# An audio tower on one core: engine orders rewritten, shorter root iterations, row hats moved to ScalarE, and setup transfers redistributed

## Chip, cores and metric

The kernel runs on 1 core of a Trainium2 chip. The metric is the device time of one execution in microseconds (us). All arithmetic that matters here is float32.

## The reference, cut to what matters

x is (128, 750, 64). Three layers follow one another; each adds to a running h of shape (128, 47, 128).

```python
# tokens: deformable convolution over w = 46 words of K = 16 taps
off  = einsum('bwkc,ock->bow', xr, w_off) + b_off
dy, dx = off[:, 0::2], off[:, 1::2]
px   = base + dx;  x0 = floor(px);  frac = px - x0
v0, v1 = gather(x0), gather(x0 + 1)                  # zero outside the row
wy   = maximum(0, 1 - abs(dy))
val  = wy * ((1 - frac) * v0 + frac * v1)
h    = concat(cls, einsum('bckw,dck->bwd', val, w_def) + b_def) + positional
# attention, one head of 128, over S = 47 tokens, on z = layernorm(h)
est  = einsum('bqkh,h->bqk', tanh(hq[:, :, None] + hk[:, None] + b1), W2[0]) + b2
h    = h + softmax(Q K^T / sqrt(128) + est) V
# experts: top 2 of 8 and a shared one, on z = layernorm(h)
h    = h + sum_e combine_e * (relu(z w1_e + b1_e) w2_e + b2_e) + relu(z sw1 + sb1) sw2 + sb2
```

The layer norm divides by sqrt(var + 1e-5). The two experts of a token are the two of highest score, ties going to the lower number.

## The kernel before, in words

The 128 sequences are cut into 16 units of 8. A unit goes through a pipeline of pieces, and at one time different units are at different stages. An engine has a list of pieces (`ORDER`) that it runs once per step; `AHEAD` says how many units ahead of (or behind) the step s the unit is on which a piece works: a, p, q, y take unit s+3, t and x unit s+4, h unit s+2, b, c, k, n unit s+1, m unit s, r unit s−1, f, g, d unit s−2. Each engine runs its list in order; between engines only semaphores hold.

The pieces that the text speaks of:

- x0 (SP) loads x of a unit, in 16 transfers (line 288). t0 to t3 (VectorE, line 535) transpose it, a3 (TensorE, line 793) makes the offsets, a3 (ScalarE, line 404) copies them out of PSUM, a4 (TensorE, line 800, the selection matmul) spreads them, and a4 (VectorE, `stage_a`, lines 543 to 563) transposes them and makes row positions, gather indices (line 551) and interpolation weights.
- GpSimd issues 36 indirect gathers per unit (line 382) for six of the eight sequences, in three blocks of 12, into one of two buffers G. c0, c1, c2 (VectorE, lines 597 to 618) combine one block each. Line 597 copies the weights to PSUM.
- The other two sequences are done without a gather: p0 (SP) writes the positions to memory, q0 (SP) reads them back spread over the partitions (PXB, WYB), h0 to h3 and k0 to k3 (ScalarE, lines 413 and 420) make hat functions of them, n0 to n3 (TensorE, line 818) multiply them with plain rows (XN, loaded by y0 on SP), and n0, n1 (VectorE, line 632, `dense_out`) scale the result.
- b3 (TensorE, line 779, sixteen matmuls, "the projection") makes the tokens of all eight sequences; b3 (VectorE, lines 642 and 643) adds the position code and gives h0.
- m0 to m5 are the first layer norm and the attention scores; m51, m52 the tanh estimates, written to memory and read back as SC by e0, e1, e2 (SP, lines 326 and 333). r6, r7 are the softmax (VectorE lines 665 to 672, ScalarE line 463), r7, r8 (TensorE) transpose and multiply by the values, r9 to r12 the second layer norm and the gate, r13 (VectorE, lines 693 to 699) the ranks of the experts, r14 the combine weights, gc their transposition.
- m1 and r10 (VectorE, `rstd`, lines 570 to 577) are the reciprocal square root of the variance: a shift of the bits gives a first value, three Newton rounds of three small instructions each refine it.
- For each expert f (TensorE line 940, ScalarE line 494) makes the hidden rows through one PSUM bank, g (TensorE line 951, VectorE line 728) scales them, d (TensorE line 963) adds them up; fs and ds are the shared expert; d8, d9 add, transpose and store the result.

The lists before:

```python
"tensor": gc n0 fs g0 n1 m0 f0 ds f1 m1 r7 f2 g1 r8 d0 m2 g2 r9 m3 f3 g3 m4 r10 m5 f4 g4 m51 d1 r11 f5 n2 g5 m52 n3
          r12 d2 f6 g6 d3 b3 f7 g7 a3 d4 a4 d5 d6 d7 d8
"scalar": gc k0 fs r6 f0 m0 f1 r7 k1 f2 k2 m3 r9 f3 m41 m4 m5 f4 m51 k3 f5 h0 m52 h1 r12 h2 f6 h3 f7 a3
"vector": r6 c0 r7 g0 m1 g1 r8 m2 n0 g2 m3 m4 g3 r10 g4 c1 r11 g5 c2 n1 r12 r13 g6 r14 b3 g7 t0 t1 a4 d8 t2 d9 t3
"sync":   x0 e0 e1 e2 p0 q0 y0 d9
```

At the start SP loads x of unit 0 and later all large constants, ScalarE's queue loads the six small ones (identity, offset weights, row bases and the like), and TensorE makes two products of attention matrices (lines 988 to 990) before it begins the first projection. GpSimd's program has a loop over pairs of units, and so has SP's.

Of the kernel before, what the change touches and what calls it, by code (L numbers as in the profile page):

```python
# [6 lines left out]
K = 16  # L7
# [30 lines left out]
ROUND = 8388608.0  # L38

CONSTS = [  # L40
    ("ident", [128, 128]), ("wof", [128, KP * 32]), ("selm", [128, 128]), ("base", [128, NBLK * 4]),
    ("boff", [128, 8]), ("rowbase", [128, GBLK]),
# [13 lines left out]
    "tensor": ("gc n0 fs g0 n1 m0 f0 ds f1 m1 r7 f2 g1 r8 d0 m2 g2 r9 m3 f3 g3 m4 r10 m5 f4 g4 m51 d1 r11 f5 n2 g5 m52 n3 "  # L56
               "r12 d2 f6 g6 d3 b3 f7 g7 a3 d4 a4 d5 d6 d7 d8").split(),
    "scalar": ("gc k0 fs r6 f0 m0 f1 r7 k1 f2 k2 m3 r9 f3 m41 m4 m5 f4 m51 k3 f5 h0 m52 h1 r12 h2 f6 h3 f7 a3").split(),
    "vector": ("r6 c0 r7 g0 m1 g1 r8 m2 n0 g2 m3 m4 g3 r10 g4 c1 r11 g5 c2 n1 r12 r13 g6 r14 b3 g7 t0 t1 a4 d8 t2 d9 t3").split(),
    "sync": ("x0 e0 e1 e2 p0 q0 y0 d9").split(),  # L60
}

END_ORDER = {}
# [9 lines left out]
class Chain:  # L73


    def __init__(self, eng, sem):
        self.eng, self.sem, self.base, self.n = eng, sem, 0, 0

    def __call__(self, ins):
        ins.then_inc(self.sem, 1)  # L80
        self.n += 1
        self.eng.wait_ge(self.sem, self.base + self.n)

    def mark(self):
        self.at = self.n

    def loop(self, i, first, per):

        self.outer = self.base + self.n
        self.base, self.n = self.outer + (i - first) * per, 0  # L90

    def end(self, trips, per):
        assert self.n == per, (self.n, per)
        self.base, self.n = self.outer + trips * per, 0


def audio_tower(nc, x, consts, rows, pw, est, out):
# [4 lines left out]
    with ctx:  # L102
# [21 lines left out]
        ones = sb("ones", [128, 128])  # L124
# [56 lines left out]
        eq = sb("eq", [RT, RN, E, E])  # L181
# [20 lines left out]
        def cols(t):  # L202
            return bank[t][:, 0:COLS]
# [13 lines left out]
        x_turned, off_full, off_ready, ot_full, ot_read, idx_ready, pw_ready = (  # L217
            sem(n) for n in ("x_turned", "off_full", "off_ready", "ot_full", "ot_read", "idx_ready", "pw_ready"))
# [18 lines left out]
        def early(engine, pieces, s):  # L237

            for name in ORDER[engine]:
                v = s + AHEAD[name[0]]  # L240
                if name in pieces and 0 <= v < UNITS:
                    pieces[name](v // 2, v % 2)

        def steps(eng, engine, pieces, chain=None, last=(UNITS - 4) // 2, loop=True):

            def step(i, t):
                for name in (END_ORDER.get(t, ORDER) if isinstance(i, int) else ORDER)[engine]:
                    v = t + AHEAD[name[0]]
                    if not isinstance(i, int):
                        pieces[name](i + v // 2, v % 2)  # L250
                    elif 0 <= v < UNITS:
                        pieces[name](v // 2, v % 2)

            if not loop:
                for s in range(-1, UNITS + 2):
                    step(0, s)
                return
            for s in (-1, 0, 1, 2):
                step(0, s)
            if chain:  # L260
                chain.mark()
            for s in (3, 4):
                step(0, s)
            per = chain.n - chain.at if chain else 0
            with eng.Fori(2, last) as i:
                if chain:
                    chain.loop(i, 2, per)
                for r in (1, 2):
                    step(i, r)
            if chain:  # L270
                chain.end(last - 2, per)
            for s in range(2 * last + 1, UNITS + 2):
                step(0, s)
# [4 lines left out]
        def _(sp):  # L278
# [16 lines left out]
            def write_positions(m, h):  # L295
# [3 lines left out]
                for r, t in ((0, nw[:, GBLK:NBLK, :]), (1, offs[:, GBLK:NBLK, 4:8])):  # L299
# [44 lines left out]
            load_x(0, 0)  # L344
# [4 lines left out]
            early("sync", pieces, -3)  # L349
            for name, _s in CONSTS[NFIRST + 1:]:  # L350
                sp.dma_start(cs[name][:, :], consts[name]).then_inc(const_in, 16)
            sp.wait_ge(zeroed, 1)
            for b in range(NB):
                sp.dma_start(w2blk[H * b:H * b + H, b:b + 1], rows["w2col"]).then_inc(blk_in, 16)
            early("sync", pieces, -2)
            steps(sp, "sync", pieces, last=(UNITS - 6) // 2)
# [4 lines left out]
        def _(pool):  # L361
            pool.memset(w2blk[:, :], 0.0).then_inc(zeroed, 1)
# [5 lines left out]
            pool.memset(ones[:, :], 1.0).then_inc(zeroed, 1)  # L368
# [18 lines left out]
            gathers(0, 0)  # L387
# [671 lines left out]
```

## Time and profile before

| | us |
|---|---|
| median of 3 runs | 860.05 (859.48 to 864.42) |
| the profiled execution, its own time | 864.31 |
| its span on the core | 862.5 |
| VectorE busy | 670.7 |
| TensorE busy (matmul) | 691.1 |
| ScalarE busy | 515.8 |
| GpSimd busy | 547.7 |

The span is that of the profiled execution from its first to its last instruction. Busy times leave out semaphore and DMA-issuing instructions and the short gaps between dependent ones. The mean granted TensorE clock was 0.956 of full speed.

### The profile page before, as it was taken

How to read it: one execution, taken by the hardware profiler on the slowest of the kernel's cores; microseconds unless marked ns; L12 is line 12 of the kernel's file. 1: busy time of each engine (PE TensorE's matmuls, PEld its weight loads, DVE VectorE, ACT ScalarE, POOL GpSimd, SP SyncE). 2: the span in 40 equal slices, each digit the busy share in tenths (PEclk: the TensorE clock that was granted, in tenths of full speed). 3: DMA queues.
4: the chain of work that ended last, by engine and by line, in shares of the span. 5: the costliest groups of instructions: out<-in, count | busy, mean ns of one | idle time of the engine just before them, and what ended most of it. 6: DMA issues, size and time to landing. Idle time of an engine off the chain costs nothing.

```text
span 862.5 us, 17862 instructions
## 1 busy us (share of the span) xinstructions
PE 691.1 (80%) x6294; PEld 416.1 (48%) x6294; DVE 670.7 (78%) x1750; ACT 515.8 (60%) x903; POOL 547.7 (63%) x588
## 2 busy tenths in 40 slices
PE   2106586879899898989898988888888999998786
PEld 0004354545465555555464645555554555555342
DVE  5146667879888988898898989898888889796552
ACT  0217565647675857767576758585775767744422
POOL 1777777777777777777777777777777777300000
PEclk9999978899989998999999999999999999999889
DMA  4877486647373747565564647475756354200101
GB/s 145 183 180 192 88 170 137 125 84 176 58 206 61 186 86 154 118 123 143 100 169 57 197 76 170 101 155 117 138 131 125 73 93 99 44 18 10 27 0 19
DMA packets 130669, 97.79 MB, mean 113 GB/s; under 512 B 87180, under 2 KB 118868, under 8 KB 130588
## 3 DMA queue, kind: packets, MB, share of 16 engines
q1 hardware_dynamic: 111292, 58.64, 26.3%
q0 software_dynamic: 18432, 37.79, 25.7%
q8 instruction: 50, 0.82, 0.4%
q10 hardware_dynamic: 864, 0.30, 0.1%
q14 instruction: 31, 0.25, 0.1%
HBM read 88.75 MB, written 7.90 MB: 112 GB/s over the span
## 4 chain that ended last, share of the span: by engine, by line
DVE 41%; PE 37%; issue 9%; ACT 5%; SPq 4%; DMA 3%; DVEq 0%; ACTq 0%
PE bank L779 8%; PE bank L940 6%; PE bank L818 5%; DVE XT L535 4%; PE bank L963 4%; DVE bank L609 4%; DVE VAL L615 4%; PE bank L854 3%; DVE G L606 3%; DVE TH L654 3%; DVE VT L632 3%; PE bank L793 2%; DVE GE L728 2%; ACT HT L413 2%; SPq L288 2%
## 5 line engine op out<-in xcount | busy, mean ns | idle before, releaser
L382 POOL DMA_INDIRECT G<-in_x,idx x576 | 545.4, 947 | 195.7 <-issue 173.7
L413 ACT ACTIVATE HT<-PXB,c_lneg 128x736 f32<-128x736 f32 x192 | 160.1, 897 | 74.4 <-PE bank L818 55.5
L818 PE MATMUL bank<-HT,XN 128*32 128x184 f32 x3072 | 137.9, 329 | 8.5 <-ACT HT L420 5.2
L940 PE MATMUL bank<-Z,c_w1e 128*128 128x376 f32 x288 | 125.9, 519 | 20.3 <-ACT HE L494 18.4
L420 ACT ACTIVATE HT<-HT 128x2208 f32<-128x2208 f32 x64 | 130.3, 2036 | 0.6
L818 PEld LDWEIGHTS bank<-HT,XN 128*32 128x32 f32 x3072 | 102.8, 113 | 42.7 <-issue 17.5
L779 PE MATMUL bank<-VT,c_wdef 128*128 128x380 f32 x256 | 87.2, 495 | 23.2 <-DVE VT L632 23.2
L963 PE MATMUL bank<-GE,c_w2e 128*128 128x376 f32 x256 | 104.4, 513 | 0.7 <-DVE GE L728 0.7
L535 DVE STREAM_TRANSPOSE XT<-xt 128x768 f32<-128x768 f32 x64 | 59.9, 958 | 54.2 <-DMA xt<-in_x 33.3
L494 ACT ACTIVATE HE<-bank,c_fb 128x376 f32<-128x376 f32 x128 | 73.0, 570 | 38.9 <-PE bank L940 37.2
L728 DVE TENSOR_TENSOR GE<-HE,bank 128x376 f32<-128x376 f32 x128 | 68.7, 537 | 34.4 <-ACT HE L494 24.7
L779 PEld LDWEIGHTS bank<-VT,c_wdef 128*128 128x128 f32 x256 | 48.1, 193 | 61.5 <-DVE VT L618 28.5
L940 PEld LDWEIGHTS bank<-Z,c_w1e 128*128 128x128 f32 x288 | 49.7, 193 | 57.4 <-ACT HE L494 31.4
L963 PEld LDWEIGHTS bank<-GE,c_w2e 128*128 128x128 f32 x256 | 45.1, 198 | 31.5 <-issue 17.5
L609 DVE TENSOR_TENSOR bank<-G,bank 128x384 f32<-128x384 f32 x96 | 54.0, 562 | 3.3
L615 DVE TENSOR_TENSOR VAL<-G,bank 128x384 f32<-128x384 f32 x96 | 53.1, 553 | 3.3
L793 PE MATMUL bank<-XT,c_wof 128*32 128x384 f32 x256 | 26.5, 536 | 30.3 <-DVE XT L535 20.3
L463 ACT ACTIVATE SC<-SC,smx 47x47 f32<-47x47 f32 x128 | 40.8, 320 | 16.5 <-DVE smx L667 16.5
L618 DVE STREAM_TRANSPOSE VT<-VAL 128x768 f32<-128x768 f32 x48 | 47.0, 978 | 1.7
L606 DVE TENSOR_TENSOR G<-G,bank 128x768 f32<-128x768 f32 x48 | 45.4, 945 | 0.6
L951 PE MATMUL bank<-cT,selb 72*128 72x376 bf16 x128 | 43.5, 340 | 0.3 <-DVE GE L728 0.2
L834 PE MATMUL bank<-h,c_center 128*128 128x376 f32 x64 | 29.1, 536 | 16.7 <-DVE smx L667 16.7
(136 smaller groups left out, 931.3 us busy)
## 6 DMA issues: line engine op xcount, KB each, us to landing
xt<-in_x SPq DMA_DIRECT2D x256, 96.0 KB
PXB<-pw SPq DMA_DIRECT2D x16, 768.0 KB
G<-in_x,idx POOLq DMA_INDIRECT x576
XN<-in_x SPq DMA_DIRECT2D x16, 384.0 KB
est<-SQHC SPq DMA_DIRECT2D x32, 141.0 KB
WYB<-pw SPq DMA_DIRECT2D x64, 48.0 KB
out<-OUTS SPq DMA_DIRECT2D x64, 44.0 KB
SC<-est SPq DMA_DIRECT2D x16, 69.0 KB
```

The costliest lines, as they stand in the source:

```text
L382: pool.indirect_dma_start(out=G[h][:, col, :], out_offset=None, in_=x.rearrange("b (l c) -> (b l) c", c=C), in_offset=bass.IndirectOffsetO ...
L413: act.activation(HT[half][:, c, :, :].rearrange("p g (w n) -> p g w n", n=4), PXB[h][:, :].rearrange("p (g w i n) -> p i g w n", g=NG, i=2 ...
L420: act.activation(rows_, rows_, ACT.Relu, bias=1.0, scale=-1.0).then_inc(hat_ready, 1)
L494: act.activation(HE[e % 4][:, :], cols(2), ACT.Relu, bias=cs["fb1"][:, e:e + 1]).then_inc(he_ready, 1)
L535: dve.transpose(XT[:, :, 96 * bp:96 * bp + 96].rearrange("p q (t i) -> p t q i", i=32), xt[:, WG * bp:WG * bp + WG, :].rearrange("p t (q i ...
L609: ins = dve.tensor_tensor(prod, G[h][:, k0 + a:k0 + b, C:2 * C], weight(1, a, b), ALU.mult)
L615: chain(dve.tensor_tensor(VAL[:, a:b, :], G[h][:, k0 + a:k0 + b, 0:C], prod, ALU.add))
L728: dve.tensor_tensor(GE[e % 4][:, :], HE[e % 4][:, :], cols(3), ALU.mult).then_inc(ge_ready, 1)
L779: mm = pe.matmul(bank[0][:, 0:TOK], wdef[:, q, :], VT[:, q, :], start=(q == 0), stop=(q == KP - 1))
L818: mm = pe.matmul(bank[0][32 * g:32 * g + 32, HW * c:HW * c + HW], XN[h][:, b, C * ch + 32 * c:C * ch + 32 * c + 32], HT[half][:, k, g, :], ...
L940: pe.matmul(cols(2), w1e[:, e, :], Z2[h][:, :], start=True, stop=True).then_inc(up_full, 1)
L963: pe.matmul(cols(4), w2e[:, e, :], HS[:, 0:COLS] if e == E else GE[e % 4][:, :], start=(e == E), stop=False).then_inc(down_done, 1)
```

## The change

1. The helpers for loops go; each engine's steps are written out, GpSimd's and SP's too.
2. All four lists have a new order.
3. `rstd`: another first guess and constants; after one round of three instructions comes one of four.
4. `stage_a`: the bias of the offsets is added by ScalarE in its copy (`Identity` with bias); the hat functions for the gathered rows go to ScalarE as a new piece a4 (`row_hats`, five activations); the sign of nw turns. The product of the weights is made in c0 straight into PSUM, in place of the copy.
5. Ranks: one comparison against a constant `least` (0 or the smallest positive number, by the place of the pair) replaces an equality, a mask and a comparison. The maximum of the softmax is negated by the reduction.
6. Setup: x of unit 0 is loaded half by SP, half by ScalarE's queue; the six small constants by GpSimd's queue; the large constants and the attention vector (29 transfers) by ScalarE's queue after its first step. The products of attention matrices come after the first projection.

```diff
 ORDER = {
+    "tensor": ("n0 fs gc g0 n1 f0 ds m0 f1 m1 r7 d0 g1 f2 r8 m2 g2 f3 m3 r9 g3 m4 d1 r10 m5 f4 m51 d2 g4 f5 m52 r11 g5 n2 "
+               "f6 r12 g6 d3 f7 g7 d4 d5 n3 d6 b3 d7 d8 a3 a4").split(),
+    "scalar": ("gc fs r6 f0 m0 k0 f1 r7 f2 k1 f3 m3 r9 m41 m4 m5 f4 m51 f5 m52 k2 f6 r12 k3 h0 h1 f7 h2 h3 a3 a4").split(),
+    "vector": ("r6 c0 r7 g0 m1 g1 r8 m2 n0 g2 m3 g3 m4 r10 g4 c1 r11 g5 r12 g6 c2 n1 r13 g7 r14 b3 d8 d9 a4 t0 t1 t2 t3").split(),
+    "sync": ("x0 y0 e0 e1 e2 p0 d9 q0").split(),
 }
...
+            def row_hats(m, h):
+                u = 2 * m + h
+                act.wait_ge(ot_read, u + 1)
...
+                act.activation(nw[h][:, :, :], offT[:, :, 0:4], ACT.Abs).then_inc(nw_abs, 1)
+                act.wait_ge(nw_abs, u + 1)
+                act.wait_ge(rest_ready, u + 1)
+                act.activation(nw[h][:, :, :], nw[h][:, :, :], ACT.Relu, bias=1.0, scale=-1.0).then_inc(pw_ready, 1)
+                for i in range(2):
+                    act.activation(e01[h][:, :, :, i], rest[:, :, :], ACT.Abs, bias=float(i)).then_inc(e_abs, 1)
+                act.wait_ge(e_abs, 2 * u + 2)
+                e = e01[h][:, :, :, :].rearrange("p t n s -> p (t n s)")
+                act.activation(e, e, ACT.Relu, bias=1.0, scale=-1.0).then_inc(e_ready, 1)
...
-                chain(dve.tensor_tensor(offs[:, :, :], offT[:, :, 0:8], cs["boff"][:, :].unsqueeze(1).broadcast_to([128, NBLK, 8]), ALU.add))
-                chain(dve.tensor_tensor(offs[:, :, 4:8], offs[:, :, 4:8], base, ALU.add))
-                pxg = offs[:, 0:GBLK, 4:8]
+                chain(dve.tensor_tensor(px[:, :, :], offT[:, :, 4:8], base, ALU.add))
+                pxg = px[:, 0:GBLK, :]
...
+                wait(dve, e_abs, 2 * u)
+                dve.scalar_tensor_tensor(rest[:, :, :], rr[:, :, :], ROUND, pxg, ALU.subtract, ALU.subtract).then_inc(rest_ready, 1)
...
-                    for _i in range(3):
-                        chain(dve.scalar_tensor_tensor(nt_[:, :], ry[:, :], -0.5, ry[:, :], ALU.mult, ALU.mult))
-                        chain(dve.tensor_tensor(nt_[:, :], nt_[:, :], var[:, :], ALU.mult))
-                        chain(dve.scalar_tensor_tensor(ry[:, :], nt_[:, :], 1.5, ry[:, :], ALU.add, ALU.mult))
+                    chain(dve.scalar_tensor_tensor(nt_[:, :], ry[:, :], -0.703952253, ry[:, :], ALU.mult, ALU.mult))
+                    chain(dve.tensor_tensor(nt_[:, :], nt_[:, :], var[:, :], ALU.mult))
+                    chain(dve.scalar_tensor_tensor(ry[:, :], nt_[:, :], 1.68191391, ry[:, :], ALU.add, ALU.mult))
+                    chain(dve.tensor_tensor(nt_[:, :], ry[:, :], ry[:, :], ALU.mult))
+                    chain(dve.tensor_tensor(nt_[:, :], nt_[:, :], var[:, :], ALU.mult))
+                    chain(dve.scalar_tensor_tensor(nt_[:, :], nt_[:, :], -10.0 / 3.0, nt_[:, :], ALU.add, ALU.mult))
+                    chain(dve.scalar_tensor_tensor(ry[:, :], nt_[:, :], 5.0, ry[:, :], ALU.add, ALU.mult))
...
-                chain(dve.reduce_max(smx[:, :], SC[:, :, 0:S], AX.X))
-                dve.tensor_scalar(smx[:, :], smx[:, :], -1.0, None, ALU.mult).then_inc(sc_ready, 1)
+                dve.tensor_reduce(smx[:, :], SC[:, :, 0:S], AX.X, ALU.max, negate=True).then_inc(sc_ready, 1)
...
-                chain(dve.scalar_tensor_tensor(eqv, gtv, 0.0, cs["tri"][0:RT, :].unsqueeze(1).broadcast_to([RT, RN, E * E]),
-                                               ALU.is_equal, ALU.mult))
-                chain(dve.scalar_tensor_tensor(gtv, gtv, 0.0, eqv, ALU.is_gt, ALU.add))
+                chain(dve.tensor_tensor(gtv, gtv, least[:, :].unsqueeze(1).broadcast_to([RT, RN, E * E]), ALU.is_ge))
...
-            early("tensor", pieces, -3)
-            early("tensor", pieces, -2)
+            steps("tensor", pieces, -3, 0)
```

## Rows read from the trace of the kernel before

**Rows 1.** The page's busy time of each engine, share, instructions.
```profile
PE 691.1 (80%) x6294; PEld 416.1 (48%) x6294; DVE 670.7 (78%) x1750; ACT 515.8 (60%) x903; POOL 547.7 (63%) x588
```
**Rows 2.** Timeline of GpSimd: start, us, what; first and last gather.
```profile
22.42 1.09 POOL L382 DMA_INDIRECT G<-in_x,idx  x1 [19.59 <-DVE idx L551]
...
742.95 0.94 POOL L382 DMA_INDIRECT G<-in_x,idx  x1 [0.30 <-issue]
```
**Rows 3.** Stretches between projections: length, busy us by engine, clock, DMA.
```profile
core 0: us, PE busy (x) PEld busy (x) DVE busy (x) ACT busy (x) POOL busy (x), PEclk, DMA share, GB/s
263.31:309.69 46.38, 40.95 (x393) 24.65 (x394) 41.18 (x109) 31.93 (x56) 35.10 (x38) 1.00 0.58 129
309.69:358.54 48.85, 43.94 (x393) 26.88 (x394) 41.48 (x109) 32.03 (x56) 36.96 (x40) 0.93 0.58 126
...
404.93:452.35 47.42, 42.30 (x394) 26.05 (x394) 41.39 (x109) 32.06 (x56) 35.84 (x39) 0.96 0.61 132
```
**Rows 4.** Timeline of TensorE, four places.
```profile
123.38 5.35 PE L779 MATMUL bank<-VT,c_wdef 128*128 128x380 f32 x16 [1.08 <-DVE VT L632]
...
411.70 1.50 PE L793 MATMUL bank<-XT,c_wof 128*32 128x384 f32 x16 [0.63 <-DVE h L643]
...
413.87 0.91 PE L800 MATMUL bank<-off,c_selm 128*128 128x384 f32 x2
...
772.96 5.34 PE L779 MATMUL bank<-VT,c_wdef 128*128 128x380 f32 x16 [1.45 <-DVE VT L632]
...
778.93 2.69 PE L963 MATMUL bank<-GE,c_w2e 128*128 128x376 f32 x8
```
**Rows 5.** VectorE's waits, 200 to 700 us: total, times, longest.
```profile
DVE GE L728 <- ACT HE L494: 15.1, 11, 1.4
DVE XT L535 <- PE bank L793: 12.4, 10, 1.2
```
**Rows 6.** Groups by line: busy us, mean ns, idle before.
```profile
L696 DVE SCALAR_TENSOR_TENSOR eq<-gt,c_tri 94x256 f32<-94x256 f32 x16 | 7.0, 437 | 0.5
...
L546 DVE TENSOR_TENSOR offs<-offT,c_boff 128x96 f32<-128x96 f32 x16 | 4.2, 262 | 0.5
...
L476 ACT ACTIVATE eg<-lg 94x32 f32<-94x32 f32 x16 | 3.7, 229 | 37.6 <-DVE lg L685 37.6
...
L556 DVE TENSOR_SCALAR nw<-nw 128x48 f32<-128x48 f32 x16 | 3.0, 188 | 0.6
...
L498 ACT ACT_TABLE_LOAD x1 | 1.3, 1283 | 4.3 <-issue 4.3
```
**Rows 7.** Timeline of VectorE within one step, 421 to 448 us.
```profile
421.85 0.56 DVE L665 SCALAR_TENSOR_TENSOR SC<-bank,c_b2col,SC 47x376 f32<-47x376 f32 x1
...
428.71 0.15 DVE L570 TENSOR_SCALAR var<-bank 94x4 f32<-94x4 f32 x1
...
431.27 0.55 DVE L577 TENSOR_TENSOR diag<-c_ident,ry 94x376 f32<-94x376 f32 x1
...
447.13 0.94 DVE L606 TENSOR_TENSOR G<-G,bank 128x768 f32<-128x768 f32 x1
```
**Rows 8.** Timeline of the start, SP's queue and VectorE.
```profile
0.76 10.41 SPq L288 DMA_DIRECT2D xt<-in_x  x16
...
6.64 0.23 DVE L525 CAST identb<-c_ident 128x128 bf16<-128x128 f32 x1 [1.43 <-DMA c_rowbase<-in_rowbase]
...
13.21 0.98 DVE L535 STREAM_TRANSPOSE XT<-xt 128x768 f32<-128x768 f32 x1 [1.05 <-DMA xt<-in_x]
```
**Rows 9.** Estimates: SP's timeline in a step, and the last read in the chain.
```profile
448.22 1.06 SPq L326 DMA_DIRECT2D est<-SQHC  x2
454.91 0.28 SPq L333 DMA_DIRECT2D SC<-est  x1
...
806.71 5.83 DMA SC<-est
```

More of the change, by code:

```diff
@@ L81, in __call__ @@
         self.n += 1
[L82 to L94, printed above, removed]
+        self.eng.wait_ge(self.sem, self.n)
 def audio_tower(nc, x, consts, rows, pw, est, out):
@@ L123, in audio_tower @@
         b2s = sb("b2s", [72, 128], bf16)
-        ones = sb("ones", [128, 128])
+        spread = sb("spread", [128, 128])
         mean1 = sb("mean1", [128, 1])
@@ L136, in audio_tower @@
         offT = sb("offT", [128, NBLK, 32])
-        offs = sb("offs", [128, NBLK, 8])
-        nw = sb("nw", [128, NBLK, 4])
+        px = sb("px", [128, NBLK, 4])
+        nw = [sb(f"nw{p}", [128, NBLK, 4]) for p in range(2)]
+        rest = sb("rest", [128, GBLK, 4])
         rr = sb("rr", [128, GBLK, 4])
-        e01 = sb("e01", [128, GBLK, 4, 2])
-        e01f = e01[:, :, :, :].rearrange("p t n s -> p (t n s)")
+        e01 = [sb(f"e01{p}", [128, GBLK, 4, 2]) for p in range(2)]
         rowb = sb("rowb", [128, GBLK])
         idx = [sb(f"idx{p}", [128, GBLK * 4], i32) for p in range(2)]
-        aw = [sb(f"aw{p}", [128, GBLK, 4, 2]) for p in range(2)]
         G = [sb(f"G{p}", [128, GBLK * 4, 2 * C]) for p in range(2)]
@@ L235, in audio_tower, with load_first, steps @@
         dve_chain, act_chain = sem("dve_chain"), sem("act_chain")
[L237 to L273, printed above, removed]
+        def load_first(eng, parts):
+            for bp in parts:
+                src = x[bass.ds(2 * bp, 2), :].rearrange("b (t w g n) -> g w b t n", t=WG, w=16, g=NG)
+                for g in range(NG):
+                    eng.dma_start(xt[32 * g:32 * g + 32, WG * bp:WG * bp + WG, :], src[g]).then_inc(x_in[bp], 16)
+        def steps(engine, pieces, first, last):
+            for s in range(first, last):
+                for name in ORDERS.get(s, ORDER)[engine]:
+                    u = s + AHEAD[name[0]]
+                    if name in pieces and 0 <= u < UNITS:
+                        pieces[name](u // 2, u % 2)
         block = ctx.enter_context(nc.Block())
@@ L348, in _ @@
                       "e0": write_estimate(0), "e1": write_estimate(1), "e2": read_estimate}
[L349 to L356, printed above, removed]
+            steps("sync", pieces, -3, UNITS + 2)
             for h in range(2):
@@ L367, in _ @@
             pool.memset(HS[:, :], 0.0).then_inc(zeroed, 1)
-            pool.memset(ones[:, :], 1.0).then_inc(zeroed, 1)
+            pool.memset(spread[:, :], 0.375).then_inc(zeroed, 1)
             pool.memset(mean1[:, :], 1.0 / D).then_inc(zeroed, 1)
@@ L385, in gathers @@
                         ).then_inc(gathered[h][bp], 16)
-            gathers(0, 0)
-            gathers(0, 1)
-            with pool.Fori(1, UNITS // 2) as i:
-                gathers(i, 0)
-                gathers(i, 1)
+            for u in range(UNITS):
+                gathers(u // 2, u % 2)
         @block.scalar
@@ L766, in _ @@
             dve.wait_ge(dve_consts, 5)
+            chain(dve.tensor_scalar(least[:, :], cs["tri"][0:RT, :], -TINY, TINY, ALU.mult, ALU.add))
             for p in range(2):
@@ L853, in piece @@
                     pe.wait_ge(diag_ready[ln], 2 * m + h + 1)
-                    pe.matmul(cols(LNB[ln]), ones[0:RT, :], diag[ln][:, :, :].rearrange("p t r -> p (t r)"),
+                    pe.matmul(cols(LNB[ln]), spread[0:RT, :], diag[ln][:, :, :].rearrange("p t r -> p (t r)"),
                               start=True, stop=True).then_inc(rstd_full[ln], 1)
@@ L991, in _ @@
             pe.wait_ge(setup_mats, 5)
-            steps(pe, "tensor", pieces, loop=False)
+            steps("tensor", pieces, 0, UNITS + 2)
 def kernel(**inputs):
```

77 lines of the change are left out of this document (37 added, 40 removed).

## The prediction

> **What bounds the kernel now.** I read five views, in this order: the busy shares, GpSimd's timeline from end to end, the table of stretches cut at the token projection (TensorE's sixteen matmuls of line 779, once per unit, a good mark for one step), VectorE's waits, and one step instruction by instruction.
>
> By the busy shares TensorE has 80%, VectorE 78%, GpSimd 63% [rows 1]. GpSimd's share misleads. It issues 576 gathers; the first starts at 22.42 and the last at 742.95 [rows 2], so one comes every (742.95 − 22.42) / 575 = 1.253 us, of which only some 0.95 counts as busy. 36 gathers a unit make 45.0 us a unit: a floor under every step that no other engine can beat, and it runs nearly without a break. A step takes 46.38 us where the granted clock was 1.00, and 47.42 and 48.85 us at 0.96 and 0.93 [rows 3]. So the engines run 1.4 us a unit behind what GpSimd would allow, and the lost time piles up: the projection of unit 1 starts at 123.38, that of unit 15 at 772.96 [rows 4], that is 649.6 us for 14 units, 46.4 each.
>
> Who sets the 46.38? VectorE is busy 41.18 us of it and some 100 small gaps between dependent instructions fill most of the rest; over 200 to 700 us it waits 15.1 us in 11 places for the experts' hidden rows and 12.4 us in 10 for the offset matmuls [rows 5], that is 2.6 us a step. TensorE is busy 40.95 us of the same step [rows 3]. So VectorE's instruction list is the bound of a step (43.8 us occupied), TensorE second (about 41), GpSimd third only in appearance: its 45.0 is a hard floor.
>
> **The change, part by part, per unit.**
> *Offsets and hats (line 543 to 563).* Seven VectorE instructions go: the bias add (0.262 us), the two of nw, four of e01; the cheapest, line 556, takes 0.188 [rows 6]. Seven at about 0.225, with 0.03 us from each end to the next start, give 1.8 us. The weights' product of line 563 takes the place of the copy of line 597, at the same price. ScalarE gets five activations of 36 to 96 elements; the nearest, 32 elements, takes 0.229 us [rows 6], so 1.2 us on an engine that is busy 31.93 of 46.38 us [rows 3]. They run after the last transposition of a step, and next behind them on ScalarE stand the copy of the combine weights and the shared hidden rows, whose matmuls are due 3 us later: hidden; without that cover 1.2 us.
> *Roots.* Twelve small instructions run from 428.71 to 431.27 [rows 7], 0.213 us each. Three rounds (9) become two of higher order (3 + 4): two fewer, 0.43 us, twice a unit: 0.86.
> *Ranks and maxima.* One 94x256 instruction goes, 0.437 us [rows 6], and the negation: 0.47 + 0.2. The comparison, written as a plain two-tensor operation, and the two products of line 632 have no reason to be dearer: nothing.
> Sum on VectorE: 1.8 + 0.86 + 0.67 = 3.3 us of 43.8, leaving 40.5. TensorE loses nothing. If all of it came off the step, a step would be 43.1 us, below GpSimd's 45.0: at least 1.9 of the 3.3 us can't show.
>
> *The new orders.* They decide the rest; I cut a step in two.
> Stretch one, from the start of the projection to VectorE's first softmax instruction, now 404.93 to 421.85: 16.9 us [rows 3, 7]. After the change: projection 5.34 [rows 4]; VectorE's adds of h0 0.8; offset matmuls, ScalarE's copy and the selection matmul 411.70 to 414.78 = 3.1 us [rows 4]; then stage_a 1.9 us (seven instructions instead of fourteen), and only then all four transposes of x, of which two now stand ahead of it and cover the offsets' round trip; they are 0.98 us each, 0.9 apart [rows 8]: 3.6. Sum 14.75, so 2.2 saved, though VectorE now idles about 2 us in front of stage_a, with the four transposes behind it.
> Stretch two, from there to the next projection: 46.38 − 16.9 = 29.5 us at full clock. Off: 0.2 + 0.43 + 0.43. On: the gate's maximum and one expert's product move from behind the third gather block to ahead of it, 0.87. Net −0.2. Today this stretch has hardly a wait at full clock [rows 5]. Walking the new lists I find new ones: VectorE at r8, because ScalarE's first hats (2.5 us) now stand ahead of f1 and of the copy that TensorE's r8 needs: 0.75; at g4, since TensorE does d2 first: 0.5; at m2 and r12 0.4. Bounds 0 and 2.5; I take 1.7, as each rests on durations of this trace. So 14.75 + 29.3 + 1.7 = 45.7 against 46.38: 0.7 us a step, ends 44.0 (then GpSimd's 45.0 holds) and 46.5. Of the 3.3 us removed 2.6 turn into waits for TensorE. The steps at a lower clock (47.42, 48.85 us) cost as much more as now: TensorE's work is the same.
>
> *Start.* The first gather waits for the first indices. x comes in 16 transfers on one queue, issued over 10.41 us, and the last block is turned at 13.21 [rows 8]; half of them on ScalarE's queue take up to 5 us off that. Against it, the constants that VectorE waits for, now there at 6.6 us, go through GpSimd's queue; nothing in the trace prices a plain transfer from there. Between 0 and 4 us earlier, I take 1.5. The Trainium skill, "DMA: Bandwidth & Descriptors", section "Specifications", gives the GpSimd path about 1 us to the first byte against 0.6 for the others; by that alone six transfers would hold the start back by about 2 us and leave less of the gain; no run here shows it yet. The 29 setup transfers move from SP to ScalarE (some 14 us of issue), behind unit 0's offsets and ahead of its hats, which wait that long for the positions to be written out and spread (PXB): hidden, and unit 0 has slack anyway, as its third gather block is not in before 67 us. Without that cover they would cost 14 us once. The setup matrices move behind the first projection; that frees TensorE's first dense matmuls.
> But the second unit is bound by GpSimd: 72 gathers end at 22.4 + 90.2 = 112.6, plus landing (0 to 5.8 us, the SC read below being the longest near; I take 2), plus 5.2 us from the third block to the projection (447.13 to 452.35 [rows 3, 7]) is 119.8, less 1.5 = 118.3 against 123.38. Unit 2 likewise: 163.4 against 168.4. Gain there 5 us, no more.
>
> *End.* Behind unit 15's projection TensorE still has eight matmuls of expert products (778.93, 2.69 us) that hold the output add and then the softmax [rows 4]; in the new order they come first: 2.5 us. Two softmax, root and rank passes shorter by 0.2 + 0.43 + 0.47 lie bare there: 1.5. Together 4.
>
> *Sum.* 5 (start) + 12 x 0.7 (units 2 to 14) + 1.5 (last short step) + 4 (end) = 19 us. Span 862.5 − 19 = 843.5; its own time 864.3 − 19 = 845.3. The median, 860.05, lies 4.3 below that execution, so I forecast 841.
>
> *The clock.* A rule that speaks against denser work: stretches of the same 393 matmuls took 46.38 us at 1.00 and 48.85 at 0.93 [rows 3], so the clock falls now and then to the lower of its levels, 1.2 GHz, in the middle of full work. The Trainium skill, "TensorE: Matmul & The Clock Gate", section "HAM oscillation — how this bites in real kernels", says that regular stalls between bursts make the clock drop again and again. By it new waits of TensorE (at r7, for the first gather block, 3 us) could cost a dip in every step, 1.0 to 2.5 us; by the rows, where TensorE idles 5.4 us of the 46.38 and keeps the full clock, nothing changes. I go by the rows.
>
> *Tables.* ScalarE's copy of the offsets becomes an Identity with a bias. One table load in the whole run, 1.283 us [rows 6]. Were Identity outside the loaded set, two loads a unit would lie on the offsets' round trip: 2.6 x 16 = 41 us. The Trainium skill, "ScalarE: Activation LUTs", section "Table sets: the hidden batching unit", says that identity, copy, relu and abs are in every set. I give the loads 1 in 100.
>
> **The rivals.**
> *GpSimd takes over (20%).* If the new waits are nearer 0.7 than 1.7, every step falls to 45.0. Then unit 15's third block starts when its last gather is in: 742.95 + 0.94 + 2 − 1.5, less GpSimd's one wait of some 1 us, about 743.3; projection 748.5 instead of 773.0; with the end's 4 that is −28.5: 831.5. For it: each wait in the walk is half a microsecond's difference between long sums. Against it: all of them would have to be wrong on the same side.
> *All of it becomes waits (17%).* Step 46.4 as before, only start and end gain: 860 − 8 = 852. For it: the offsets' round trip lies bare on VectorE, and TensorE must be waited for after the projection.
> *The estimate's round trip, slower than before (6%).* SP's y0 (the load of XN) now stands ahead of e0, e1, e2, and it waits for n1, late in the step. So the write and read of the estimates start only there: 0.5 + 1.1 (two writes, 448.22), 5.6 us until the read is issued (454.91), and 5.8 us until it lands [rows 9]: 13.0 us, while VectorE wants them 14.75 us after n1. It decides from 14.75 on: each us more per step costs 12 to 13 us. With 3 us more, as loaded queues could bring, 841 + 38 = 879. Today the writes go out 4 us before the projection (448.22 against 452.35). Against it: the heavy loads of x are over by then.
>
> **How the numbers follow.** Forecast 841 has 55%, with 837 to 848 as its own range; the rest (2%) is tables and the unforeseen. The range reaches down to the rival of GpSimd, 831, and up past 852 to a step 0.3 us longer, 857. A measurement of this kernel tells 1% (8.6 us) from nothing. Faster by more: 0.55 + 0.20 + a little of the second rival = 0.78; within: 0.15; slower: 0.07.
>
> **What would show it.** Step length at full clock 45.7 (45.0: first rival; 46.4: second); VectorE busy down by some 48 us to about 620, with waits before stage_a (2 us each) in place of the hidden-row waits; GpSimd's first gather near 21 and its last near 741.5; unit 15's projection near 758; no wait of the softmax add for the SC read (third rival: one in each step). I am wrong if that wait appears, if ScalarE's five activations hold TensorE at the shared rows, or if there is more than one table load.

## The result: slower by 1.25%, and the profile after

The changed kernel took 872.47 us (median, 869.75 to 875.39), the kernel before 860.91 on the same chip (859.48 to 865.72): a ratio of 1.0125, interval 1.0103 to 1.0148. The forecast was 841 us, with a range up to 857. The profiled execution after has a span of 870.7 us against 862.5, 8.2 more.

The page's busy time of each engine (it answers to [rows 1]):

```profile
PE 704.6 (81%) x6294; PEld 412.8 (47%) x6294; DVE 628.7 (72%) x1543; ACT 535.8 (62%) x983; POOL 553.4 (64%) x594
```

VectorE lost 42 us (forecast 48) and the run became longer: the first sign that VectorE's work wasn't what the time came from. Next the table of stretches cut at the token projection, now line 748 (beside [rows 3]):

```profile
268.41:314.80 46.39, 41.40 (x394) 24.17 (x394) 38.76 (x96) 33.14 (x62) 35.06 (x37) 1.00 0.71 129
412.05:458.08 46.03, 41.40 (x393) 24.17 (x394) 38.88 (x96) 33.12 (x62) 34.85 (x37) 1.00 0.63 130
458.08:507.21 49.13, 44.18 (x394) 26.45 (x394) 38.56 (x96) 33.26 (x62) 37.14 (x40) 0.93 0.62 125
603.12:653.56 50.44, 44.48 (x394) 26.03 (x394) 38.71 (x96) 33.25 (x62) 35.94 (x39) 0.93 0.61 120
```

A step at full clock takes 46.0, hardly less than the 46.38 of before, and the slowest 50.44. Marks along the run show where the 8.2 us arose. The projection of unit 3 starts at 219.33 (before 214.72): 4.6 late. The ten steps from there to 699.55 take 480.2 (before 471.6, 214.72 to 686.28): 8.7 more. The next two take 88.1 against 86.7: 1.4 more. From unit 15's projection to the end there are 83.05 us (787.65 to 870.7), before 89.5: 6.5 less. The sum is +8.2.

VectorE's waits from 200 to 700 us (total, times, longest; beside [rows 5]):

```profile
DVE offT L521 <- PE bank L769: 19.8, 10, 2.0
DVE h L650 <- PE bank L881: 10.7, 6, 2.3
DVE h L616 <- PE bank L748: 10.1, 10, 1.1
DVE GE L698 <- PE bank L920: 9.0, 10, 1.2
...
DVE SC L639 <- DMA SC<-est: 6.8, 6, 1.9
```

The first line is the offsets' round trip that no transpose covers, 1.98 us in each step, forecast as 2. The last is the wait that the prediction named as a sign that it is wrong. One step, first SP's timeline, then VectorE's (start, us, what; they answer to [rows 9] and [rows 7]):

```profile
411.93 0.40 SPq L284 DMA_DIRECT2D XN<-in_x  x1
412.38 1.05 SPq L292 DMA_DIRECT2D est<-SQHC  x2
420.47 0.25 SPq L299 DMA_DIRECT2D SC<-est  x1
```

```profile
421.43 0.58 DVE L521 STREAM_TRANSPOSE offT<-bank 128x384 f32<-128x384 f32 x1 [1.98 <-PE bank L769]
...
423.23 3.56 DVE L512 STREAM_TRANSPOSE XT<-xt 128x768 f32<-128x768 f32 x4
427.00 0.60 DVE L639 SCALAR_TENSOR_TENSOR SC<-bank,c_b2col,SC 47x376 f32<-47x376 f32 x1 [0.21 <-DMA SC<-est]
...
619.71 0.60 DVE L639 SCALAR_TENSOR_TENSOR SC<-bank,c_b2col,SC 47x376 f32<-47x376 f32 x1 [1.93 <-DMA SC<-est]
```

From y0 to the addition pass 427.00 − 411.93 = 15.07 us; from the first write to the issue of the read 8.09, before 6.69 [rows 9]. Over the whole run this wait makes 13.0 us in 9 places.

The start, from four timelines (GpSimd's first constant and last constant, VectorE, GpSimd's first gather; beside [rows 8] and [rows 2]), and two places of unit 0 and unit 1:

```profile
1.27 0.72 POOL L322 DMA_DIRECT2D c_wof<-in_wof  x1 [0.82 <-POOLq L1016]
...
4.11 0.56 POOL L323 DMA_DIRECT2D c_ident<-in_ident  x1
```

```profile
10.65 0.23 DVE L502 CAST identb<-c_ident 128x128 bf16<-128x128 f32 x1 [5.45 <-DMA c_ident<-in_ident]
...
116.59 0.95 DVE L580 TENSOR_TENSOR G<-G,bank 128x768 f32<-128x768 f32 x1 [2.09 <-DMA G<-in_x,idx]
```

```profile
22.14 1.01 POOL L344 DMA_INDIRECT G<-in_x,idx  x1 [15.37 <-DVE idx L528]
...
112.81 0.94 POOL L344 DMA_INDIRECT G<-in_x,idx  x1 [0.30 <-issue]
```

```profile
120.53 0.74 PE L787 MATMUL bank<-HT,XN 128*32 128x184 f32 x8 [3.12 <-ACT HT L392]
```

```profile
12.41 2.70 DVE L512 STREAM_TRANSPOSE XT<-xt 128x768 f32<-128x768 f32 x3 [0.44 <-DMA xt<-in_x]
...
124.35 0.87 DVE L606 TENSOR_TENSOR VT<-bank,WYB 128x184 f32<-128x184 f32 x2 [3.43 <-PE bank L787]
```

The identity is used at 10.65 where it was used at 6.64, and the first gather starts only 0.28 us earlier. The second transpose of x still has to wait for x at 12.41. In unit 1 TensorE's n3 waits for ScalarE's hats, and VectorE's last scaling (line 606) waits 3.43 us for TensorE, right ahead of the projection.

Last the clock, in windows of 2.5 us behind one projection (same columns as the stretches):

```profile
236.83:239.33 2.50, 0.69 (x3) 0.10 (x1) 2.36 (x5) 2.50 (x14) 1.89 (x3) 1.00 1.11 65
239.33:241.83 2.50, 2.26 (x14) 1.92 (x14) 2.40 (x7) 2.50 (x5) 1.89 (x3) 0.66 0.78 100
241.83:244.33 2.50, 2.50 (x7) 1.36 (x6) 2.19 (x11) 1.48 (x4) 1.89 (x3) 0.50 0.97 307
...
285.91:288.41 2.50, 0.94 (x3) 0.30 (x2) 2.34 (x5) 2.50 (x14) 1.89 (x2) 1.00 1.10 80
```

It falls to 0.50 (the lower of its levels, 1.2 GHz) right behind a stretch in which TensorE was busy 0.69 us of 2.50. The kernel before has the same kind of fall, behind 1.53 of 2.50 us. A thin stretch doesn't always bring a fall: at the same place of the next step (last row) TensorE is busy 0.94 of 2.50 us, and that step keeps the full clock. Of the ten middle steps three have the full clock throughout, before five.

### The profile page after: what moved, and what is told of

Read it like the earlier page. It is cut to its first block, busy times and chain, and to the rows that moved or that the text cites. A ratio compares the mean times of both kernels' runs of the same rounds, so it can differ in the third digit from the quotient of the medians.

```text
span 870.7 us, 17175 instructions
## 1 busy us (share of the span) xinstructions
PE 704.6 (81%) x6294; PEld 412.8 (47%) x6294; DVE 628.7 (72%) x1543; ACT 535.8 (62%) x983; POOL 553.4 (64%) x594
## 4 chain that ended last, share of the span: by engine, by line
PE 35%; DVE 29%; DMA 16%; issue 8%; ACT 8%; SPq 3%; DVEq 0%; ACTq 0%
DMA SC<-est 7%; DMA est<-SQHC 6%; PE bank L909 5%; PE bank L748 5%; DVE bank L583 5%; DVE VAL L589 5%; PE bank L932 4%; DVE G L580 4%; DVE XT L512 3%; PE bank L881 2%; ACT HT L385 2%; DVE GE L698 2%; PE bank L787 2%; ACT SC L435 2%; PE bank L823 2%
## 5 line engine op out<-in xcount | busy, mean ns | idle before, releaser
L909 PE MATMUL bank<-Z,c_w1e 128*128 128x376 f32 x288 | 129.8, 534 | 26.8 <-ACT HE L466 25.2
L787 PEld LDWEIGHTS bank<-HT,XN 128*32 128x32 f32 x3072 | 97.2, 114 | 74.2 <-DVE offT L521 18.6
L932 PE MATMUL bank<-GE,c_w2e 128*128 128x376 f32 x256 | 107.0, 514 | 0.0
L512 DVE STREAM_TRANSPOSE XT<-xt 128x768 f32<-128x768 f32 x64 | 57.1, 947 | 3.1 <-DMA xt<-in_x 2.6
L521 DVE STREAM_TRANSPOSE offT<-bank 128x384 f32<-128x384 f32 x16 | 9.3, 583 | 65.0 <-PE bank L769 65.0
```

What stands on the lines that cost most here:

```text
L512: dve.transpose(XT[:, :, 96 * bp:96 * bp + 96].rearrange("p q (t i) -> p t q i", i=32), xt[:, WG * bp:WG * bp + WG, :].rearrange("p t (q i ...
L787: mm = pe.matmul(bank[0][32 * g:32 * g + 32, HW * c:HW * c + HW], XN[h][:, b, C * ch + 32 * c:C * ch + 32 * c + 32], HT[half][:, k, g, :], ...
L909: pe.matmul(cols(2), w1e[:, e, :], Z2[h][:, :], start=True, stop=True).then_inc(up_full, 1)
L932: pe.matmul(cols(4), w2e[:, e, :], HS[:, 0:COLS] if e == E else GE[e % 4][:, :], start=(e == E), stop=False).then_inc(down_done, 1)
```

## The experiments

Line numbers are those of the changed kernel except where a kernel starts from the old one. My first theory: the new lists, not the arithmetic, cost the time, through y0 ahead of the estimates and through the bare offset round trip. Its rivals: the arithmetic itself (ScalarE's hats, the added rounds), the setup, or GpSimd as the bound whatever the lists.

**First set of runs: two single orders and two crossings.** A crossing sets the lists of one kernel in the other.

```diff
 a_y0_last (changed kernel)
-    "sync": ("x0 y0 e0 e1 e2 p0 d9 q0").split(),
+    "sync": ("x0 e0 e1 e2 p0 d9 q0 y0").split(),
 b_y0_first (kernel before)
-    "sync": x0 e0 e1 e2 p0 q0 y0 d9
+    "sync": x0 y0 e0 e1 e2 p0 q0 d9
 a_old_lists: the changed kernel, all four lists of before (and a4 last on ScalarE)
 b_new_lists: the kernel before, all four new lists (without ScalarE's a4)
```

> The changed kernel with one edit: SP's list has y0 (the load of XN) last again, behind q0, instead of second. Theory 1, the estimates' round trip behind y0 costs the time: the 13.0 us of waits of VectorE's softmax add for the SC read (9 times) vanish, and with them some 10 to 13 us: 859 to 862 us. Theory 2, the lower TensorE clock (0.93 against 0.956) has its own cause, the new waits of TensorE: the waits vanish but the steps at a low clock stay: 866 to 870 us. Theory 3, the softmax waits are only where other lateness shows: no change, 871 to 873.

> The kernel before with one edit: SP's list has y0 second, ahead of e0, e1, e2. Theory 1 (the round trip is what costs): its softmax add comes 16.9 us after the projection began, 2 us later than in the changed kernel (14.9), and the round trip takes about 14 to 16 us, so hardly any wait: 861 to 864 us. If y0 ahead of the estimates hurts whatever the rest of the order, 870 us or more.

> The changed kernel with the four lists of before (ScalarE's with a4 added at its end): the arithmetic and setup changes alone. VectorE's list, 43.8 us occupied of 46.4, is shortened by 3.3 us: if the lists are at fault, a step falls to GpSimd's 45.0 us, and the time to 840 to 846 us. If the arithmetic or the setup is at fault, it stays at 860 or above.

> The kernel before with the new lists and its own arithmetic and setup. VectorE does 3.3 us more per step than in the changed kernel, of which about 1 us falls into its new wait before stage_a: if the lists are at fault it is slower than both, 890 to 910 us. If the setup or the arithmetic is at fault, about 860.

Measured against the kernel before: 1.0121, 0.9988, 0.9997 and 1.0107. None of these numbers says what it was meant to: on this chip the kernel before itself took 1574.05 us, some 93 us a step. Once in a step most engines stand still for some 46 us. Here are ScalarE and TensorE in b_y0_first, and GpSimd and ScalarE in a_asis, the unedited changed kernel on another chip of this kind (third set):

```profile
752.09 0.47 PE L818 MATMUL bank<-HT,XN 128*32 128x184 f32 x1 [2.33 <-issue]
...
753.51 2.50 ACT L413 ACTIVATE HT<-PXB,c_lneg 128x736 f32<-128x736 f32 x3 [46.39 <-remote]
```

```profile
624.17 0.95 POOL L344 DMA_INDIRECT G<-in_x,idx  x1 [49.55 <-DVE idx L528]
...
676.26 0.57 ACT L466 ACTIVATE HE<-bank,c_fb 128x376 f32<-128x376 f32 x1 [45.38 <-remote]
```

While GpSimd issues its gathers (45 us), the rest hardly moves: TensorE starts single matmuls with pauses of up to 2.33 us in which it waits for nothing that the profile shows. Then GpSimd waits as long for new indices. What releases ScalarE is called "remote", which means that the profile doesn't show it. At line 413 ScalarE reads the positions that come back from memory (PXB), but at line 466 it doesn't; so their read-back, which some expectations below blame, isn't shown to be the cause. The cause stays open. All but b_y0_first were run again.

**Second set.**

> The changed kernel with y0 last in SP's list, again, on another chip. Theory 1, the estimates' round trip behind y0: its 13 us of waits vanish and so do 10 to 13 us of the time, 859 to 862 us. Theory 2, the lower TensorE clock has its own cause, TensorE's new waits: the waits vanish, the many steps at a low clock stay, 866 to 870 us.

> The changed kernel with the four old lists, again, on another chip: arithmetic and setup alone. If the lists are at fault: steps of 45.0 us (GpSimd's floor), 840 to 846 us. If the arithmetic or the setup is: 860 or more.

> The kernel before with the new lists, again, on another chip. If the lists are at fault: slower than the changed kernel, 885 to 905 us, as VectorE still has 3.3 us more in each step. If they aren't: about 860.

Two changes of one thing each: y0, and the transposes that cover the offsets' round trip again.

```diff
 a_cover = a_y0_last, and in "vector":
-  ... r14 b3 d8 d9 a4 t0 t1 t2 t3
+  ... r14 b3 t0 t1 a4 d8 t2 d9 t3
```

> The changed kernel with y0 last and, in VectorE's list, the offsets' round trip covered again: t0 t1 a4 d8 t2 d9 t3 in place of d8 d9 a4 t0 t1 t2 t3. VectorE's 2.0 us of wait before stage_a should vanish and a full-clock step fall from 46.0 to GpSimd's 45.0 us. By theory 1: 845 to 850 us. By theory 2, which has the clock follow TensorE's waits, the gain over a_y0_last is less than 5 us.

| | us (before 868.33) | ratio | interval |
|---|---|---|---|
| a_y0_last_2 | 862.15 | 0.9944 | 0.9920 to 0.9968 |
| a_cover | 850.78 | 0.9813 | 0.9781 to 0.9844 |
| a_old_lists_2 | 845.88 | 0.9775 | 0.9739 to 0.9811 |
| b_new_lists_2 | 914.66 | 1.0564 | 1.0521 to 1.0606 |

The crossing decides. The arithmetic and the setup under the old lists gain 2.25%; the new lists under the old arithmetic lose 5.6%, more than the 885 to 905 us expected. Under the changed arithmetic the new lists cost 16.3 us on this chip (862.15 with y0 last against 845.88). Stretches of a_old_lists_2, a_cover and b_new_lists_2, one near the same place of each:

```profile
255.91:300.48 44.57, 40.93 (x394) 24.64 (x394) 38.27 (x96) 32.65 (x61) 33.59 (x37) 1.00 0.63 134
```

```profile
404.98:450.14 45.16, 41.40 (x393) 24.16 (x394) 38.46 (x96) 33.13 (x62) 34.37 (x36) 1.00 0.71 131
```

```profile
331.18:380.40 49.22, 43.00 (x394) 24.97 (x394) 42.03 (x109) 32.05 (x57) 34.06 (x36) 0.97 0.60 121
```

Under the old lists a step falls to GpSimd's floor: 45.1 us in the mean of ten (36 times 1.253 is 45.1), with single steps of 43.6 made up for by longer ones, and between 200 and 700 us GpSimd never waits for indices. Its timeline at the end and VectorE's last block of unit 15 (a_old_lists_2):

```profile
743.67 0.94 POOL L344 DMA_INDIRECT G<-in_x,idx  x1 [0.30 <-issue]
```

```profile
746.43 0.95 DVE L580 TENSOR_TENSOR G<-G,bank 128x768 f32<-128x768 f32 x1 [0.79 <-DMA G<-in_x,idx]
```

That is the rival "GpSimd takes over" in its mechanism. Its numbers were too low: unit 15's projection starts at 751.66, not 748.5, and the end is not the shorter one of the new lists, so that the gain is 22.5 us against the kernel before and not 28.5. Under the new lists with the old arithmetic no step of the middle part is under 49.2, and GpSimd waits for indices (40.1 us in 8 places between 200 and 700). The stage_a of before has fourteen instructions where the changed one has seven, and in these lists all of them lie bare behind the offsets' round trip.

a_cover against a_y0_last_2 is one move in one list: 1.3%, 11.4 us, where theory 2 allowed less than 5. So this move alone, two transposes over the offsets' round trip, brings back 11.4 of the 16.3 us. At full clock the step falls from 45.8 to 45.25 us in the mean. Part of what is won goes to a new wait: the transposes that now come early must wait until the matmuls of line 762 have read XT (16.9 us in 10 places between 200 and 700).

**Third set**, again a chip on which every version takes about twice as long (the kernel before 1565.57). The expectations were written before this was known.

```diff
 a_asis: the changed kernel, unedited
 a_old_y0 = a_old_lists with "sync": x0 y0 e0 e1 e2 p0 q0 d9
 a_best = a_old_lists, and
-ORDERS = {}
+ORDERS = {s: LATE for s in range(14, 18)}
 (LATE holds the four new lists)
 a_cover_n1 = a_cover, and in "tensor":
-  n0 fs gc g0 n1 f0 ds m0 f1 m1 r7 d0
+  n0 fs gc g0 f0 ds m0 f1 m1 n1 r7 d0
```

> The changed kernel itself, unedited, beside the others on one chip, so that what y0 costs is known on the same footing. Ratio to the kernel before 1.0125 as measured first. Against the 0.9944 of the version with y0 last that leaves 1.8%, 15.6 us, for y0's place. If the difference between chips made it, it comes nearer to 1.00.

> The old lists with the changed arithmetic, with y0 second in SP's list. Theory 1, the price of y0's place depends on how soon the softmax add comes after the projection (16 to 17 us in the old lists, 14.9 in the new ones, for a round trip of about 15 to 16): nearly free here, ratio 0.978 to 0.982. Rival: y0 costs its 1.8% in any order, as the round trip is on the path of each step: ratio 0.995.

> The old lists with the changed arithmetic in steps up to 13, and the new lists in the last four steps, where there are no more gathers to wait for. Projection of unit 15 to the end took 88.9 us with the old lists and 83.1 with the new: if that end is worth what it looks, 6 us off, ratio 0.9705, about 840 us beside 868 of before. Rival: the gain of the end was the step before it being late anyway: 0.977 as without it.

> a_cover with one edit in TensorE's list: the second dense piece n1 (2 us) moves from behind g0 to just ahead of r7, into the thinnest stretch of a step, where TensorE waits for the softmax and after which the clock was seen to fall. Theory of the clock: with the stretch filled the dips go (clock 0.95 and more, steps all near 45.2), ratio 0.970 to 0.975. Rival, the idle time only moves ahead of m0 and the dips with it: 0.981 as a_cover.

Measured: 1.0105, 0.9991, 0.9985, 0.9905. They tell nothing of the step under test: a step is made up of other waits here, and among the versions with the new lists one is 1% longer than the kernel before and one 1% shorter.

**Fourth set, the same four.**

> The changed kernel, unedited, again, on a chip where the positions are read back at the normal speed. Ratio to before 1.0125 as first measured, so that y0's place is worth 1.8% (15.6 us). If a difference between chips made it: nearer to 1.00.

> Old lists, changed arithmetic, y0 second in SP's list, again. If y0's price depends on how soon the softmax add follows the projection: 0.978 to 0.982, nearly free. If it costs 1.8% in any order: 0.995.

> Old lists up to step 13, new lists for the last four steps, again. If the new lists' end is worth its 6 us: 0.9705. If not: 0.9775.

> a_cover with TensorE's n1 moved to just ahead of r7, again. If the clock falls because of that thin stretch: 0.970 to 0.975, clock 0.95 or more. If the idle time only moves: 0.981.

| | us (before 861.36) | ratio | interval |
|---|---|---|---|
| a_asis_2 | 862.62 | 1.0012 | 0.9988 to 1.0036 |
| a_old_y0_2 | 845.61 | 0.9810 | 0.9783 to 0.9837 |
| a_best_2 | 838.96 | 0.9744 | 0.9717 to 0.9772 |
| a_cover_n1_2 | 866.18 | 1.0062 | 1.0040 to 1.0083 |

The unedited kernel is not slower here. Against it the same arithmetic under the old lists, with y0 in the same place, gains 17.0 us on the same chip (862.62 to 845.61). y0 ahead of the estimates costs the old lists some 0.35% by comparison over two chips (0.9810, 0.9775; the intervals overlap), with no wait for SC between 200 and 700 us. a_best is the fastest version: old lists up to step 13 and the new ones for the last four. From its projection of unit 15 (753.70) to the end pass 82.5 us, with the old lists throughout 88.9 (a_old_lists_2: 751.66 to 840.6): so the new order of the end is worth 6.4 us in these two traces. The times say less: 0.9744 lies between the 0.9705 and the 0.9775 that were expected, 0.3% below a_old_lists_2 on the other chip.

a_cover_n1 tests a theory of the clock: that it falls because TensorE runs thin ahead of r7, so n1's matmuls are moved there. The move made it 2.5% slower than a_cover (1.0062 against 0.9813, on two chips), with full-clock steps of 46.0 to 46.5, and more steps with a fall, not fewer. TensorE's waits from 200 to 700, a_cover first, a_cover_n1_2 second:

```profile
PE bank L909 <- ACT HE L466: 2.1, 7, 0.4
```

```profile
PE bank L909 <- ACT HE L466: 20.3, 10, 2.2
```

The idle time wasn't filled but moved ahead of f1 and grew. The theory fell in this form, its rival (0.981) too, and what sets the falls stays open.

**Fifth set: the changed kernel and y0 last, on one chip.**

> The changed kernel unedited, on the same chip as the next run, which the earlier runs of the two never were. If the place of y0 costs what the two results on different chips say (1.012 for the changed kernel on its first chip, 0.994 with y0 last on another), it is 1.8% slower than the next run; if what the second chip of the changed kernel says (1.001), 0.7%.

> The changed kernel with only y0 moved behind e0 e1 e2. Full-clock step 45.7 to 46.0 us, no wait of the softmax's addition for the estimates above 0.3 us in most steps; 0.994 of the kernel before as on its first chip. Against the changed kernel on this same chip: 0.7% faster by the one reading, 1.8% by the other; and if most of the 1.8% was the chip and not the order, the two stand within 0.5%.

Against 866.88 of before: a_asis_3 861.84, ratio 0.9960 (0.9935 to 0.9986); a_y0_last_3 860.62, 0.9945 (0.9915 to 0.9975). The two stand 0.15% apart, which can't be told from nothing: the price of 1.8% that a comparison over chips had suggested isn't there on this chip. On the first chip y0 last was never run, so what its place cost there isn't shown. SP's timeline of one step of a_asis_3, VectorE's addition behind it, and VectorE's wait for it between 200 and 700:

```profile
409.08 1.05 SPq L292 DMA_DIRECT2D est<-SQHC  x2
416.54 0.25 SPq L299 DMA_DIRECT2D SC<-est  x1
```

```profile
423.44 0.56 DVE L639 SCALAR_TENSOR_TENSOR SC<-bank,c_b2col,SC 47x376 f32<-47x376 f32 x1
```

```profile
DVE SC L639 <- DMA SC<-est: 0.9, 1, 0.9
```

Here 7.46 us pass from write to read, not 8.09, and the addition doesn't wait. Over the eleven steps from 200 to 700 us the interval is 7.0 to 7.7 (a_asis_3) and 7.1 to 8.0 (a_asis_2); in the first ten of after it was 7.4 to 8.6. The order leaves the trip hardly any slack, so half a microsecond more or less decides whether the addition waits. Two stretches of a_asis_3:

```profile
454.55:500.16 45.61, 41.40 (x393) 24.16 (x394) 38.45 (x96) 33.11 (x62) 34.51 (x37) 1.00 0.64 132
500.16:548.66 48.50, 44.30 (x394) 26.20 (x394) 38.65 (x96) 33.23 (x62) 36.62 (x40) 0.93 0.63 126
```

Of my first theory the lists stand: they take the gain, mainly by the offsets' round trip that nothing covers (a_cover). y0's place shows no price on this last chip.

## Why the prediction was wrong

**What held.** The removed work: VectorE's busy time fell by 42 us to 628.7 (forecast 48, to about 620). The 2 us ahead of stage_a, in every step. The walk through the new lists: 45.7 at full clock, measured 45.6 to 45.8 in a_asis_3, 45.6 to 46.0 in a_y0_last_2, and 46.0 to 46.4 on the first chip. Stretch one of the step shown, 427.00 − 412.05 = 14.95 (forecast 14.75). One table load. The end: 6.5 us gained, forecast 4 (its two shorter passes, at 1.1 us each, should have counted 2.2 and not 1.5).

**The step that failed: "The steps at a lower clock (47.42, 48.85 us) cost as much more as now".** I forecast the step's change from its full-clock form and carried it over to the others by this sentence. Grouped by granted clock, the ten middle steps say otherwise. How much longer than a full-clock step one takes, in the mean:

| | at 0.96 | at 0.93 | steps of ten below full clock |
|---|---|---|---|
| before | 1.0 us | 2.3 us | 5 |
| after | 2.0 | 3.2 | 7 |
| a_asis_2 | 1.5 | 3.0 | 5 |
| a_asis_3 | 1.3 | 3.3 | 5 |
| a_old_lists_2 | 0.9 | 2.3 | 5 |
| a_old_y0_2 | 1.2 | 1.9 | 5 |

TensorE has the same matmuls in all of them, and yet a fall costs more under the new lists with the new arithmetic than in the kernel before or under the old lists (where a step held by GpSimd can also make up for the one before it); on the first chip there were more falls too. Which wait makes a fall dearer isn't shown. The mean of the ten exceeds the step at full clock (46.38, 46.03, 45.7) by 0.8 us before, 2.0 after and 1.2 in a_asis_3. So of the 0.7 us a step that I forecast, and that is there at full clock, 0.2 to 0.4 is left in the mean on two other chips (46.93 and 46.77 against 47.16), and on the first chip it is a loss of 0.9. Each trace is one execution, and those of a_asis_2 spread from 854.77 to 867.44 us, so the 0.2 to 0.4 is not safe.

The rule that I weighed and set aside, in the Trainium skill's "TensorE: Matmul & The Clock Gate", section "HAM oscillation — how this bites in real kernels", would have new stalls bring more falls of the clock. The granted clock over whole executions was indeed lower: median 0.931 to 0.940 for the changed kernel, 0.951 to 0.956 before (three chips each). But with the changed arithmetic under the old lists it was 0.929 and 0.944, as low, at 845.61 and 845.88 us. So a lower clock doesn't set the new lists apart, and that the stalls are its cause isn't shown.

**The start, forecast 5 us gained.** The first gather came 0.28 us earlier, not 1.5. x was issued by 6.31 instead of 11.17, but its blocks weren't used sooner: the second transpose waited for x until 12.41, where before the first two had ended by 8.98, and the last one ended at 15.11 and not at 14.19. The gather still came a little earlier because no transposes and fewer instructions stand between the offsets and the indices. The six constants from GpSimd's queue are issued in 3.4 us and the identity is used 4.0 us later than before. The Trainium skill, "DMA: Bandwidth & Descriptors", section "Specifications", with about 1 us to the first byte against 0.6, gives the direction; the 4.0 us is far more than my 2 us from it. It held up only the first transpose, though, behind which VectorE waited for x anyway.

The projection of unit 1 I had forecast at 118.3; it started at 125.37. Of the 7.1 us, 1.4 are the later gathers: 112.81 is the first issue of the next unit, so the last of unit 1 began at 111.56 and ended at 112.5, not 111.1. Another 2.1 are the landing: its block was combined at 116.59, 4.1 later, where I took 2. The remaining 3.6 are a wait that my sum doesn't have at all, the 3.43 us for TensorE's n3, which had itself waited 3.12 us for ScalarE's hats. TensorE waits 2.0 to 3.1 us for these hats in after and in all six traces of the second, fourth and fifth sets that have the changed arithmetic under the new lists; in the two with the old lists, a_old_lists_2 and a_old_y0_2, it doesn't. VectorE's wait behind it differs from none (a_cover_n1_2) to 4.7 us (a_asis_3). There the same arithmetic and setup reach unit 1's projection at 120.50 and unit 3's at 211.32 (a_old_lists_2), against 123.38 and 214.72 before, so 2.9 and 3.4 us were there; the new lists, by 125.37 and 219.33, give back 8.0 by unit 3. On one chip, the fourth set's, it is less: 216.19 (a_asis_2) against 212.72 (a_old_y0_2). In the steps of units 1 and 2 the granted clock is 0.78 and 0.82 (before 0.82 and 0.85), and my walk was made at full clock.

**The estimate's round trip, a rival with 6%.** Its mechanism was right and its threshold nearly so (14.75), its length too short: 13.0 us forecast, 15.07 measured, made of 0.45 for y0, 8.09 from write to read where I had 1.1 + 5.6, and 6.53 to the addition where I had 5.8. I had taken the 5.6 from steps in which no load of XN was issued right ahead. I mis-summed its price as well: 3 us more make 16.0, which is 1.25 over the 14.75, and at 12 to 13 us each that is some 16 us and not 38. Measured, the addition waits 13.0 us in the trace of the first chip, 5.0 and 5.8 in those of two others. In the ten middle steps it explains directly 6.8 − 0.9 = 5.9 of the 10.9 us by which after is longer than a_asis_3 (480.2 against 469.3); GpSimd's waits for indices (11.2 against 0.3) and the clock (three full steps of ten, there five) come with it, but no run separates the three.

**The sum, term by term,** from the profiles of before and a_asis_3 (858.1 of 862.5): up to unit 3 +4.9 (forecast −5.7); middle ten −2.2 (−7); the next two −0.2 (−2.2, the short step's 1.5 among it); end −6.9 (−4). That is −4.4 where I had −19. On the first chip it is +8.2: of the 27.1 us between forecast and result there, 10.3 arose up to unit 3, 15.7 in the middle ten steps and 3.6 in the next two, while the end gave 2.5 more than I had. So 1.25% slower is partly the first chip's figure. The changed kernel took 872.47, 862.62 and 861.84 us on three chips and the kernel before 860.91, 861.36 and 866.88; the step from 1.0012 to 0.9960 is thus the kernel before, slower on the third. What holds on every chip is that the 2.2% which were forecast are missing, and that the lists took them: with the old ones they are there (0.9775, 0.9810), as the first rival had it, GpSimd as the floor.

**Weights.** "GpSimd takes over" (20%) is true of the arithmetic and not of the change; "all of it becomes waits" (17%) describes the other chips best, less its start gain. I had given the slower side 7% although two terms, the trip of 13.0 against 14.75 and the start, rested on the shortest rows that I could find.

## What to carry to other kernels

Cross the parts of a change before you explain it: arithmetic under the old order and the old arithmetic under the new order, two runs, told more here (−2.25% and +5.6%) than any reading of the profile after. A saving on one engine comes out only up to the next floor, here the 45.1 us of the gathers, and a new order that leaves a memory round trip under 1 us of slack lets a wait come and go between chips (13.0, 5.0 and 5.8 us here). Compare two versions on the same chip: the kernel before alone took 860.05 to 868.33 us in its sets at normal speed. When a step is walked at full clock, price the steps in which the clock falls apart from the rest, and the filling of the pipeline too, where other engines are late.

## What was not expected of the hardware

A plain transfer issued by GpSimd takes 0.55 to 0.72 us of its queue, and the identity, issued at 4.11, was in use only at 10.65; before, from ScalarE's queue, it was issued at 0.75 and in use at 6.64. Issuing x in about half the time didn't bring its second block in sooner: issued by 6.31 as a whole, waited for until 12.41, where before the first two transposes had ended by 8.98. The same two writes and one read through memory took 7.0 to 7.7 us from write to read on one chip and 7.4 to 8.6 on another, with the same kernel. The same fall of the clock (a step at 0.93) made a step 1.9 to 2.3 us longer under the old lists and 3.0 to 3.3 us under the new ones. And on two chips every version took 1551 to 1593 us, in the traces above with the gathers and the rest of a step one after the other instead of side by side; the profile doesn't show why.
